# Narrow products in strips of the array, a router with its weights stationary, and a new order of the steps, in a convolution-attention-experts kernel

## The reference, cut to what matters

```python
# temporal attention: E is 16 x 16 per image; only two products with it are needed
E = softmax_over_rows(V_e @ sigmoid(lhs @ rhs + b_e))        # x_tat = x @ E
lhs2 = (x_tat @ W1) @ W2                                      # 256 x 16
rhs2 = W3 . x_tat                                             # 16 x 256
# spatial attention: scores of low rank 16, 256 x 256 per image
S = softmax(V_s @ sigmoid(lhs2 @ rhs2 + b_s))
# linear attention: what the second half of the tokens needs of the first is a 16 x 16 sum per head
S_h = sum_l phi(k)[l] (x) v[l]
# router: 16 logits for each of 512 tokens of a pair, top 2 of 4 groups, top 4 experts
logits = xf @ router_w.T; scores = sigmoid(logits)
```

## Time and profile before

| what | value |
|---|---|
| median of 3 runs | 931.17 us (930.77 to 931.88) |
| the profiled execution, its own time | 933.24 us |
| its span in the profile | 931.3 us |
| PE busy | 892.2 us, 96% of the span |
| PEld, DVE, ACT, POOL busy | 787.5, 623.1, 445.6, 228.6 us |

### The profile page before, as it was taken

How to read it: one execution, slowest core, us unless ns; L and a number is a source line. 1 busy time by engine, 2 the same in 40 slices (tenths; PEclk the granted TensorE clock), 3 DMA queues, 4 the chain that set the end, 5 groups by cost and what they waited for, 6 DMA issues and landing times.

```text
span 931.3 us, 19454 instructions
## 1 busy us (share of the span) xinstructions
PE 892.2 (96%) x7824; PEld 787.5 (85%) x7824; DVE 623.1 (67%) x1637; ACT 445.6 (48%) x845; POOL 228.6 (25%) x198
## 2 busy tenths in 40 slices
PE   5998788999999999999999999999999999999997
PEld 3676666998988989889898989888898898998997
DVE  6456876887697468864797467963788547864522
ACT  3443444552574436743565526744466424732432
POOL 2013200123311224112421234112241134122232
PEclk9998899999999999999999999999999999999999
DMA  7000230030002010111002010010102100120121
GB/s 234 1 2 1 65 131 1 1 103 28 23 19 79 25 46 13 40 58 34 25 12 73 25 45 24 25 61 23 46 13 59 39 13 24 37 72 26 37 67 34
DMA packets 37961, 39.21 MB, mean 42 GB/s; under 512 B 5232, under 2 KB 34416, under 8 KB 37872
## 3 DMA queue, kind: packets, MB, share of 16 engines
q1 hardware_dynamic: 37872, 37.96, 13.0%
HBM read 32.97 MB, written 4.98 MB: 41 GB/s over the span
## 4 chain that ended last, share of the span: by engine, by line
PE 83%; DVE 8%; ACT 4%; issue 2%; DMA 1%; POOL 0%; SPq 0%; POOLq 0%; DVEq 0%; ACTq 0%
PE ring L1365 9%; PE d_ps L521 5%; PE g_ps L521 4%; PE d_ps L523 4%; PE d_ps L522 4%; PE g_ps L523 4%; PE u_ps L523 4%; PE g_ps L522 4%; PE u_ps L522 4%; PE u_ps L521 4%; PE ring L1233 4%; PE num L1262 3%; PE ring L521 3%; PE ring L1348 3%; PE ring L523 3%; PE ring L522 3%
## 5 line engine op out<-in xcount | busy, mean ns | idle before, releaser
L707 POOL TENSOR_TENSOR hl<-hb,hh 128x512 fp32r<-128x512 f32 x96 | 126.0, 1313 | 424.4 <-ACT hh L838 424.4
L838 ACT ACTIVATE hh<-hb 128x512 fp32r<-128x512 f32 x96 | 60.7, 632 | 143.5 <-DVE hb L1205 119.0
L1200 DVE TENSOR_TENSOR hb<-sl,u_ps 128x512 f32<-128x512 f32 x88 | 60.3, 685 | 93.3 <-issue 37.6
L521 PE MATMUL d_ps<-hh,down_h 128*128 128x256 f32 x384 | 116.6, 304 | 2.7 <-POOL hl L707 2.7
L522 PE MATMUL d_ps<-hl,down_h 128*128 128x256 f32 x384 | 107.8, 281 | 0.0
L523 PE MATMUL d_ps<-hh,down_l 128*128 128x256 f32 x384 | 107.6, 280 | 0.0
L521 PE MATMUL g_ps<-normed_h,gate_h 128*128 128x256 f32 x352 | 105.7, 300 | 1.1 <-DVE hb L1200 0.8
L1087 DVE TENSOR_TENSOR shared<-ring,constants 128x512 f32<-128x512 f32 x128 | 79.4, 683 | 34.1 <-PE ring L1233 34.1
L523 PE MATMUL g_ps<-normed_h,gate_l 128*128 128x256 f32 x352 | 99.2, 282 | 0.0
L523 PE MATMUL u_ps<-normed_h,up_l 128*128 128x256 f32 x352 | 99.0, 281 | 0.0
L522 PE MATMUL u_ps<-normed_l,up_h 128*128 128x256 f32 x352 | 98.8, 281 | 0.0
(11 more groups left out here) (401 smaller groups left out, 2134.7 us busy)
## 6 DMA issues: line engine op xcount, KB each, us to landing
weights_over_hidden<-weights_by_expert SPq DMA_DIRECT2D x128, 128.0 KB, 3.0
shared<-denominators_by_head SPq DMA_DIRECT2D x16, 256.0 KB
out_x<-kept SPq DMA_DIRECT2D x16, 256.0 KB, 2.2
x_s<-in_x SPq DMA_DIRECT2D x12, 256.0 KB, 3.1
raw_weights<-in_gateT SPq DMA_DIRECT2D x4, 384.0 KB, 7.1
raw_weights<-in_upT SPq DMA_DIRECT2D x4, 384.0 KB, 6.2
raw_weights<-in_down SPq DMA_DIRECT2D x4, 384.0 KB, 9.1
cheb_s<-in_cheb SPq DMA_DIRECT2D x3, 256.0 KB, 5.6
```

Of the source, the lines that this page charges most:

```text
L521: eng.matmul(ps, wh, xh, start=start, stop=False, **how)
L707: pool.tensor_tensor(hl[:, j % 2, :], hb, hh[:, j % 2, :].bitcast(F32), ALU.subtract).then_inc(*ffn_pool.mark(p, f"lo{j}"))
L838: act.activation(hh[:, j % 2, :], hb, ACT.Copy).then_inc(*ffn_act.mark(p, f"hi{j}"))
L1200: dve.tensor_tensor(hb, sl, gate_up(p, j)[1][:, :], ALU.mult).then_inc(*ffn_dve.mark(p, f"h{j}"))
```

## The change

Five edits and three new lists.

1. `Erep`: the factor `iw1` (identity and W1) comes ready from the host, once on partitions 0 to 15 and once on 64 to 79. The second image's E is written to partitions 64 to 79 (two operations of DVE, `ET0` and `ET1`, for one), so that the four products alternate between two strips of rows and fill two banks. DVE scales each bank by itself (four operations for two). Three copies of DVE at the start fall away.
2. `p2`: the two factors are laid on four strips of 32 partitions (ACT makes five copies for three), and the four products each use a strip and a bank of their own. DVE adds b_s in four operations of 256 columns for two of 512.
3. `kv`: for each 128 x 128 product there are four of 32 x 32, one in each column strip; DVE spreads the 32 columns over 128 with the mask.
4. `lg`: the router's weights (128 x 32) are stationary in four column strips and the tokens move, as fp32 in place of fp32r. ACT copies the 128 x 128 result to `logit_parts`, and a new step `lt` turns it and adds the parts with one product by a constant `sums` (128 x 64). ACT takes exp(-x) from there. The two operations of DVE fall away.
5. `OPENING`, `BODY` and `CLOSING` are written anew.

```diff
 BODY = """
-    +1 tok0 tok1 lg +1 gn +1 nrm +3 xg +1 r1 xl0 xl1 xT0 +1 r2 M +2 k0 xT1 k1 r3 +2 Y0 +1 prod v1 silu r4
-    Epre cb Eexp q0 v0 kt q1 +2 Erep dent +1 kv lr rd +2 S00 +2 V00 S01 +1 p2 at0 +1 V01 S10 +2 sp0 +1 rv0 +1
...
+    +1 tok0 +1 gn tok1 +4 lg +1 nrm xg +1 lt r1 xl0 xl1 xT0 M r2 +2 xT1 k0 k1 +1 r3 silu +1 Y0 +1 prod r4 cb
+    v1 Epre Eexp q0 v0 kt q1 +2 Erep dent +1 lr kv +1 rd +1 S00 +2 p2 V00 +2 S01 +2 sp0 at0 V01 rv0 S10 +2
...
 def banks_of(name):
-    return [f"{name}_{j}" for j in range({"S": 4, "Y": 4, "p2": 2}.get(name if name == "p2" else "" if name == "rd" else name[0], 0))] or [name]
+    return [f"{name}_{j}" for j in range({"S": 4, "Y": 4, "p2": 4, "Erep": 2}.get(name if name in ("p2", "Erep") else "" if name == "rd" else name[0], 0))] or [name]
...
                 if name == "lr":
                     act.activation(g.l2, t[:, 0:N], ACT.Copy).then_inc(*conv_act.mark(p, "l2"))
                     for b in range(2):
-                        act.activation(g.r2[64 * b:64 * b + T, :], t[64 * b + 32:64 * b + 32 + T, 0:N], ACT.Copy).then_inc(*conv_act.mark(p, f"r2{b}"))
+                        low, high = slice(64 * b, 64 * b + T), slice(64 * b + 32, 64 * b + 32 + T)
+                        act.activation(g.r2[low, 0:P], t[high, 0:P], ACT.Copy).then_inc(*conv_act.mark(p, f"r2{b}"))
+                        act.activation(g.r2[high, :], t[low, 0:N], ACT.Copy).then_inc(*conv_act.mark(p, f"l3{b}"))
...
                 if name == "lg":
-                    act.wait_ge(route_dve.of(p), route_dve.at(p, "logits"))
-                    act.activation(sc[:, :, :], sc[:, :, :], ACT.Exp, scale=-1.0).then_inc(*route_act.mark(p, "eneg"))
+                    act.wait_ge(route_pe.of(p), route_pe.at(p, "lg"))
+                    act.activation(logit_parts, num[:, 0:P], ACT.Copy).then_inc(*route_act.mark(p, "lgs"))
+                if name == "lt":
+                    act.wait_ge(route_pe.of(p), route_pe.at(p, "lt"))
+                    act.activation(sc[:, :, :].rearrange("p q e -> p (q e)"), num[:, P:P + 4 * EXPERTS], ACT.Exp, scale=-1.0).then_inc(*route_act.mark(p, "eneg"))
...
-                    for b in range(2):
-                        for c in range(2):
-                            o = (2 * b + c) * 32
-                            last = pe.matmul(t[:, o:o + 17], g.eTx[:, b, 8 * c:8 * c + 8].rearrange("p j f -> p (j f)"), iw1[:, 0:17], start=True, stop=True)
+                    for c in range(2):
+                        for b in range(2):
+                            rows = slice(64 * b, 64 * b + T)
+                            last = pe.matmul(tile(p, f"Erep_{b}")[:, 32 * c:32 * c + 17], g.eTx[rows, 8 * c:8 * c + 8].rearrange("p j f -> p (j f)"), small_at("iw1")[rows, 0:17],
+                                             start=True, stop=True, tile_position=(64 * b, 0))
...
-                    for m in range(2):
-                        for b in range(2):
-                            rows = slice(64 * b, 64 * b + T)
-                            last = pe.matmul(tile(p, f"p2_{b}")[:, m * N:(m + 1) * N], g.r2[rows, m * P:(m + 1) * P], g.l2[rows, :], start=True, stop=True,
-                                             tile_position=(64 * b, 0))
+                    for b in range(2):
+                        for m in range(2):
+                            rows = slice(64 * b + 32 * m, 64 * b + 32 * m + T)
+                            right, left = (g.l2[rows, P:N], g.r2[rows, :]) if m else (g.r2[rows, 0:P], g.l2[rows, :])
+                            last = pe.matmul(tile(p, f"p2_{2 * b + m}")[:, 0:N], right, left, start=True, stop=True, tile_position=(64 * b + 32 * m, 0))
...
-                            heads_of = v_s[:, b, 0, 4 * c:4 * c + 4, :].rearrange("p j (s e) -> p j s e", e=16)[:, :, 0:3:2, :]
-                            last = pe.matmul(t[:, q * P:(q + 1) * P].rearrange("p (j s e) -> p j s e", j=4, s=2), ktok[:, q * P:(q + 1) * P], heads_of, start=True, stop=True)
+                            for j in range(4):
+                                heads_of = v_s[:, b, 0, 4 * c + j, :].rearrange("p (s e) -> p s e", e=16)[:, 0:3:2, :]
+                                last = pe.matmul(t[32 * j:32 * j + 32, 32 * q:32 * q + 32].rearrange("p (s e) -> p s e", s=2), ktok[:, q * P + 32 * j:q * P + 32 * j + 32], heads_of,
+                                                 start=True, stop=True, tile_position=(0, 32 * j))
...
+                    for k in range(2):
+                        both = router[:, k].rearrange("p s e -> p (s e)").bitcast(F32)
+                        for part, normed in enumerate((normed_h[p % 2], normed_l[p % 2])):
+                            for q in range(4):
+                                last = pe.matmul(num[32 * q:32 * q + 32, 0:P], both, normed[:, k, q * P:(q + 1) * P].bitcast(F32), start=(k == 0 and part == 0), stop=(k == 1 and part == 1),
+                                                 skip_group_check=True, tile_position=(0, 32 * q))
+                    last.then_inc(*route_pe.mark(p, name))
+                if name == "lt":
+                    pe.wait_ge(route_act.of(p), route_act.at(p, "lgs"))
+                    pe.matmul(num[:, P:P + 4 * EXPERTS], logit_parts, const_at("sums"), start=True, stop=True, skip_group_check=True).then_inc(*route_pe.mark(p, name))
```

More of the change, by code:

```diff
@@ L83 @@
     "attn": ("tok0 tok1 nrm xl0 xl1 k0 k1 v0 v1 q0 q1 kt kv dent rd S00 V00 S01 V01 S10 at0 V10 S11 V11 at1 wo0 wo1 exp").split(),
[L84 removed]
+    "route": "tk0 tk1 nrm2 xn0 xn1 lg lt r1 r2 r3 r4 cb silu".split(),
 }
@@ L130 @@
-    +1 1:xl1 2:tc0 0:r3 0:silu +1 2:tc1 +1 0:r4 1:k0 1:k1 +1 0:cb 1:v1 2:xb 1:q0 1:v0 1:kt 1:q1 +2 0:low12 +1
-    1:dent 1:kv +1 1:rd 0:high13 +2 1:S00 +2 0:exp +1 0:low13 +1 1:V00 1:S01 +5 2:z1 +1 1:at0 +2 1:V01 1:S10
-    +3 1:V10 +2 1:S11 +2 2:z2 +2 1:V11 +1 1:at1 +1 2:z3 +1 1:wo0 +3 1:wo1 +1 1:exp +1 1:tk0 1:tk1 +2 1:nrm2
-    +4 1:xn0 1:xn1 +1
+    0:hot0 0:gn 0:xg 0:hot1 0:xT0 1:gn 1:xg 0:M 0:hot2 0:xT1 1:xT0 0:Y0 2:gn 0:prod 1:M 1:xT1 0:Epre 0:hot3
+    0:Eexp 2:xg 1:Y0 0:high0 1:prod 0:Erep 0:hot4 0:lr 1:Epre 0:low0 2:xT0 0:p2 1:Eexp 0:sp0 1:Erep 0:rv0
@@ L141 @@
+    v1 Epre Eexp q0 v0 kt q1 +2 Erep dent +1 lr kv +1 rd +1 S00 +2 p2 V00 +2 S01 +2 sp0 at0 V01 rv0 S10 +2
+    sp1 st0 +1 rv1 Y1 +4 st1 o0 o1 +2 tc0 xb tc1 +1 z1 V10 S11 +2 V11 +4 at1 z2 wo0 +1 wo1 z3 +2 tk0 tk1 +4
+    nrm2 +2 xn0 xn1 +1 exp
 """
 CLOSING = """
[L144 to L146 removed]
@@ L147 @@
-    7:r3 +1 7:silu 7:r4 +1 7:cb +30 7:exp +17
+    +1 7:tok0 6:lg 7:tok1 +2 6:lt +1 7:nrm 6:r1 +2 6:r2 +2 7:xl0 +1 7:xl1 +3 6:r3 6:silu 6:r4 6:cb 7:k0 7:k1
+    7:v1 7:q0 7:v0 7:kt 7:q1 +3 7:dent 7:kv +3 7:rd 7:S00 +1 7:V00 7:S01 +2 7:at0 7:V01 7:S10 +2 7:V10 7:S11
+    +3 7:V11 7:at1 +1 7:wo0 +1 7:wo1 +1 7:tk0 +2 7:tk1 +4 7:nrm2 +4 7:xn0 7:xn1 +2 7:lg +2 7:lt +1 7:r1 +3
+    7:r2 +4 7:r3 +1 7:silu 7:r4 7:cb +27 7:exp +24
 """
```

121 lines of the change are left out of this document (58 added, 63 removed).

## The result

The changed kernel takes 940.81 us (median of 4 runs, 936.37 to 941.86), the kernel before 930.97 beside it (4 runs, 927.44 to 931.88): ratio 1.0104, 95% interval 1.0062 to 1.0146. It is slower, as forecast, but by 9.8 us and not by 3.3, outside the range of 921.5 to 939. And the time isn't lost where I placed it.

A forecast was written before the change was run, and what follows sets the result against it. PE was taken to bound the kernel, busy 107.5 of 107.8 us in a turn. Five turns +5.5, opening -1.5 and closing -0.7 made +3.3 us, a median of 934.5, range 921.5 to 939.

The forecast's parts named there:

- the term for the opening: Before the first turn: smaller PE blocks and shorter list against `at0` 0.8 later; -1.5 us, between -5 and +4.
- the shorter list behind it wins back some 2: In the opening, behind pair 0's `at0`: the shorter step list was to recover some 2 us.
- the late weight pieces cost more than I grant: Rival, opening: `at0` holds `S10`'s masks on DVE; with `k0` only 2 us earlier, opening +3, median 939. Chance 0.15, inside slower's 0.48.
- The body: The five repeated turns: new waits outweigh PE's savings, a turn 108.7 us instead of 107.6, five turns +5.5.
- a turn under 107.2: Sign in the changed profile, between two `tok0`: a turn this short in us would show the forecast wrong.
- place 3: In a turn, `lr` now ahead of `kv`: PE waits 1.1 us for DVE's scaling of `Erep`, behind the late weights.
- place 2: In a turn, exp(-x) reaches DVE late, at T+11.8: PE waits 0.4 us at `k0` and 0.2 at `prod`'s addition.
- Place 1: In a turn, `gn` between the token tiles: PE waits 0.45 us for DVE's statistics.
- Place 4: In a turn, `S10` behind `sp0`: PE waits 0.4 us until ACT's exp has read the shared fourth bank.
- The added work off PE costs nothing beyond this: In a turn: ACT's added copies and DVE's two additions in `p2` stay hidden; without cover, 0.3 and 0.8 us a turn.
- the savings arrive and the waits don't: Rival: if `r1` starts before T+10.7, `lr` finds its input; turn 105.9 to 106.7 us, total 920.5 to 924.5. Chance 0.28.
- The closing: After the five turns: `kv` once and `lg` twice save 0.9 us, two short waits of `V` cost 0.2; -0.7.

The follow-up runs named there:

- late_pieces_last: The changed kernel with its late weight pieces issued on the DMA queue behind pair 0's denominators instead of ahead of them: 928.18 us, 0.998 of the kernel before.

## Why the prediction was right and wrong

**The step that failed** is the term for the opening, "with `k0` 5.5 us earlier, `at0` is 0.8 later": I took -1.5 us for the opening, it measured +13.0. The mechanism stood in it, with `z3`, SP and the pieces, and its interval too: `at0` 31.5 us after `k0` forecast, 31.98 measured. But `k0` was not 5.5 us earlier. It started at 113.24 instead of 110.83, and at 110.36 to 112.60 in six other profiles with the same instructions up to there (110.49 in late_pieces_last). `xl0` does come 4.4 us earlier on PE (99.4 against 103.8), and then `k0` stands on DVE behind `z1` and `z2` of pair 1, which the new list left ahead of it. I moved a step forward by what PE had won and didn't ask where DVE was. That makes `at0` 9.2 us later and not 0.8. Two more things made it worse, and neither was in the sum. While `at0` waits, PE idles 7 us, and behind that it runs in part at 1.2 GHz: from `at0` to `tk0` it took 21.1 us (18.1 before), 2.7 of it the clock. And "the shorter list behind it wins back some 2" didn't happen: from `tk0` to the first turn it took 95.2 us (94.5 before). The rival "the late weight pieces cost more than I grant" was this case. It had 0.15 and +3, and its price is mis-sized for the same reason: it let `k0` be 2 us earlier at worst. (Its own sum is off as well: -1.5 and the 3.5 that `k0` loses make +2 and a median of 938, not +3 and 939.) With the queue in the other order the opening is 1.0 us shorter than before (247.54 against 248.55), close to the -1.5.

**The body** is the second term that failed: it was forecast at +1.1 us a turn, +5.5 for five, and measured -0.6 a turn, -3.4 for five; "a turn under 107.2" was to show it wrong, and 107.07 does. What failed in it is above all place 3, the wait of 1.1 us for `lr`, which was 0.22; then the waits of place 2 (0.6 together), of which none came, and the block of `kv`, 0.55 too long. Its steps one by one, blocks as start to start:

- `lg` and `lt`: 1.18 us (1.01 and 0.17) for 1.78, saving 0.60; I said 0.4. Undone, it costs 1.2 a turn.
- `Erep`: 0.55, as forecast.
- `p2`: 0.65, forecast 0.6.
- `kv`: 403.71 to 404.11, 0.40 us for 32 instructions; I said 0.95, near the upper end. This is the largest error in a block: 12.5 ns each. The floor of the Trainium skill that I cited (TensorE: Matmul & The Clock Gate, Part 1: 25 ns from start to start, so 0.8 us) doesn't hold for these products in four strips, and the measurement decides. Another part of the same page of the Trainium skill (Part 3, Measured speedup vs the span model) has some 4 ns for each packed tile, and I should have weighed that one.
- Place 1, `gn`: 0.34, forecast 0.45. Right.
- Place 2: `r1` at T+11.5 (forecast 11.8), right; but no wait at `k0` or `Epre`, for DVE made the way from `r1` to `prod`'s addition in 12.4 us, not 13.4.
- Place 3, `lr`: 0.22, forecast 1.1. In order of time on DVE, with T = 368.40:

```profile
379.88 0.20 DVE L1138 TENSOR_SCALAR sc<-sc 128x64 f32<-128x64 f32 x1 [0.57 <-ACT sc L835]
...
392.24 0.17 DVE L937 TENSOR_TENSOR conv_small<-ring,small_parameters 16x32 f32<-16x32 f32 x1
...
394.45 0.25 DVE L1133 STREAM_TRANSPOSE turned_weights<-pairs 128x64 f32<-128x64 f32 x1
...
401.35 0.69 DVE L1208 TENSOR_TENSOR hb<-hb,weights_over_hidden 128x512 f32<-128x512 f32 x1
...
402.38 0.18 DVE L972 TENSOR_TENSOR conv_small<-small_parameters,ring 128x32 f32<-128x32 f32 x1
```

  `cb` ends at T+26.3 (forecast 27.5), the first use of the weights starts 6.65 later (forecast 6.9), with DVE busy and not waiting for the transfer, and the scaling is done at T+34.2 (forecast 35.8). The chain is the right one, 1.6 us too long: 0.3 up to `r1`, 1.0 of the way to `prod`, 0.2 of the way to the weights, and 0.2 in the scaling.
- Place 4, `S10`: 0.47, forecast 0.4. Right.
- A fifth wait that I had costed at nothing: `S00`, 0.73, for the copies of ACT behind `lr` (404.50 to 406.26, five instead of three). "The added work off PE costs nothing beyond this" is wrong there.

Savings of 2.1 us, where the prediction has 1.5, and waits of 1.8 make -0.6 with the 0.3 that PE idled before. The rival "the savings arrive and the waits don't" was nearly true of the body, and by the wrong condition: `r1` was late, as forecast, and it did not matter.

**The closing**, from its `tok0` to the end, gave -0.8 for -0.7. Right.

**Direction and chances.** Slower had the highest chance and came, by another mechanism than the one that had the 0.48. That is luck: the sum +3.3 was 5.5 - 1.5 - 0.7, and it measured -3.4 + 13.0 - 0.8, so that the errors of two terms, -8.9 and +14.5, partly cancel. Five turns of +1.1 did not exist; with the pieces behind the denominators the same change is a small gain (0.998 of the kernel before), and with p2 left as it was one of 0.3%.

**What stays open.** How the 12.6 us divide is read from two profiles only, and 2.75 us between them lie ahead of `k0`, within what two openings differ by. Why the kernel before is slower with its pieces later was not tried further. That the low clock of the early opening follows from PE's waits is read from the rows and not shown by an experiment; what it costs has no number. `Erep` was not undone alone.
